# Routing by expert choice: the router product with its matrix held in TensorE, and the threshold search with the next two candidates made ahead

## The reference, cut to what matters

```python
xt = layernorm(x).reshape(N, D)                 # N = 8192, D = 128
scores = softmax(xt @ Wr, axis=-1)              # Wr: 128 x 8
G, idx = top_k(scores.T, k)                     # k = 2048 tokens of each expert
X_in = xt[idx]
h = gelu(einsum('ekd,edh->ekh', X_in, W1) + b1)
X_e = einsum('ekh,ehd->ekd', h, W2) + b2
out = zeros.at[idx].add(G * X_e)
```

## Time and profile before

| | |
|---|---|
| median of 3 runs | 3967.55 us (3966.43 to 3967.9) |
| the profiled execution, its own time | 3959.59 us |
| its span in the profile | 3957.4 us |
| its mean granted TensorE clock | 0.94 of full speed |
| TensorE busy over the span | 3411.8 us (86%) |
| VectorE busy | 2894.6 us (73%) |
| ScalarE busy | 1895.0 us (48%) |
| GpSimd busy | 1550.7 us (39%) |

### The profile page before, as it was taken

One profiled execution on the slowest core, in us unless ns is written; L12 is line 12 of the kernel. 1 busy time (PEld: TensorE's weight loads), 2 busy tenths in 40 slices (PEclk: granted clock), 3 DMA queues, 4 the chain that ended last, 5 costly groups with the idle time before them and its releaser, 6 DMA issues. The chain is left out here.

```text
span 3957.4 us, 60589 instructions
## 1 busy us (share of the span) xinstructions
PE 3411.8 (86%) x21076; PEld 2116.3 (53%) x21076; DVE 2894.6 (73%) x6400; ACT 1895.0 (48%) x3447; POOL 1550.7 (39%) x1015
## 2 busy tenths in 40 slices
PE   5999999878999984677748888888886999999987
PEld 3666666555777764344423333333333666666653
DVE  7888888556777755533239999999997777777765
ACT  2555556324665650222237676776673333333325
POOL 2311111542211200588848878878873011111112
PEclk9999999998999995798969999999998999999999
DMA  6333332004444424233332332322322222222211
GB/s 151 94 89 90 89 89 57 1 5 113 101 101 103 98 62 123 58 43 44 42 79 73 95 99 83 94 78 73 95 78 60 90 87 87 87 87 87 88 59 43
DMA packets 242528, 314.18 MB, mean 79 GB/s; under 512 B 46450, under 2 KB 157779, under 8 KB 231588
## 3 DMA queue, kind: packets, MB, share of 16 engines
q1 hardware_dynamic: 208308, 289.02, 26.6%
q0 software_dynamic: 22528, 17.32, 3.3%
q10 hardware_dynamic: 11392, 3.97, 0.5%
HBM read 251.93 MB, written 57.08 MB: 78 GB/s over the span
## 5 line engine op out<-in xcount | busy, mean ns | idle before, releaser
L574 DVE TENSOR_REDUCE a_Mx<-a_Sx 128x2 f32<-128x512 f32 (+1 forms) x1024 | 590.2, 617 | 173.4 <-PE a_Sx L626 128.0
L2187 POOL TENSOR_TENSOR a_inp<-a_dtu,a_Bs 128x1024 f32<-128x1024 f32 x256 | 598.0, 2361 | 68.6 <-DMA a_Bs<-a_brows 43.4
L2465 DVE TENSOR_TENSOR_SCAN a_h<-a_dA,a_inp 128x1024 f32<-128x1024 f32 x256 | 583.0, 2283 | 32.1 <-ACT a_dA L2348 28.7
L2592 PE MATMUL a_Y<-a_hc,g_ident 128*128 128x512 f32 x1024 | 487.6, 599 | 5.4 <-POOL a_hc L2201 3.6
L347 POOL TENSOR_TENSOR a_rest<-a_qk,a_parts 128x512 f32<-128x512 f32 x64 | 75.3, 1176 | 917.0 <-ACT a_parts L399 917.0
L413 ACT ACTIVATE a_Pr<-a_SA 128x512 f32<-128x512 f32 x512 | 305.1, 596 | 167.7 <-DVE a_SA L524 79.6
L623 PE MATMUL a_Sx<-att_Kp,att_Qp 96*128 96x256 bf16 (+1 forms) x2048 | 345.8, 261 | 41.4 <-DMA att_Qp<-a_crows 18.1
L2348 ACT ACTIVATE a_dA<-a_dtA,a_A 128x512 f32<-128x512 f32 x512 | 329.8, 681 | 97.8 <-DVE a_h L2465 96.8
L1937 ACT ACTIVATE f_sg<-f_GB 128x512 f32<-128x512 f32 x272 | 162.7, 598 | 436.5 <-PE f_GB L2013 436.3
L2063 PEld LDWEIGHTS f_OUT<-g_routed_wd,f_hm 128*128 128x128 f32 x2176 | 280.6, 191 | 124.1 <-issue 90.5
L2592 PEld LDWEIGHTS a_Y<-a_hc,g_ident 128*128 128x128 f32 x1024 | 195.4, 194 | 234.0 <-issue 222.7
(11 more groups left out here) (474 smaller groups left out, 6803.3 us busy)
## 6 DMA issues: line engine op xcount, KB each, us to landing
a_Bs<-a_brows SPq DMA_DIRECT2D x256, 256.0 KB, 3.3
f_Cs<-f_crows SPq DMA_DIRECT2D x512, 128.0 KB, 2.9
att_Qp<-a_packing SPq DMA_DIRECT2D x192, 192.0 KB
att_Kp<-a_packing SPq DMA_DIRECT2D x192, 192.0 KB
a_packing<-a_parts SPq DMA_DIRECT2D x64, 384.0 KB, 2.8
a_packing<-a_parts SPq DMA_DIRECT2D x64, 128.0 KB, 2.8
a_Cs<-a_brows SPq DMA_DIRECT2D x32, 256.0 KB, 4.7
g_x<-x SPq DMA_DIRECT2D x8, 512.0 KB, 7.4
```

The source lines that it names most:

```text
L574: nc.vector.tensor_reduce(Mx[(k + 2 - (j < LATE)) % 2][:, t, 2 * jj:2 * jj + 2], Sx[t][:, 0:2 * wd].rearrange("p (h q) -> p h q", h=2), AX ...
L2187: nc.gpsimd.tensor_tensor(inp[n % Q][:], dtu[k][:], Bs[n % Q][:].unsqueeze(1).to_broadcast([P, CH, GT]), ALU.mult).then_inc(s["mulB"], 1)
L2465: nc.vector.tensor_tensor_scan(h[n % 2][:].rearrange("p c q -> p (c q)"), dA[m % 2][:].rearrange("p c q -> p (c q)"), inp[n % Q][:].rearra ...
L2592: nc.tensor.matmul(Y[c][:], ident[:], hc[n % Q][:, c], start=False, stop=(n == N - 1))\
```

## The change

In the router, the roles of the two operands are exchanged. `wr` (128 rows, 8 columns) becomes the stationary operand and the 512 tokens of `xnT` are streamed past it in one matmul into a new PSUM tile `LT` of 8 partitions x 512. ScalarE copies `LT` into a new SBUF tile `rows`. TensorE turns the four 8 x 128 pieces of `rows` back with four transposes against the 8 x 8 corner of the identity, into the old places of `LG`, one step later than the old matmuls were. VectorE's copy of `LG` moves by one step too, and the loops of both engines get one step more (`back=1`).

In `choose`, there are two buffers `cand`. While the counts of one candidate are being added, VectorE brings `kth` up to date for the bit before (`copy_predicated`), and makes both next candidates: `high`, for the case that the bit is taken, and the other `cand` buffer, for the case that it isn't. When the sum is there, it makes the mask and copies `high` over the new candidate where the mask is set.

```diff
+        LT = [sc.ps(f"LT{i}", [E, GT]) for i in range(2)]
+        rows = [sc.sb(f"rows{i}", [E, GT]) for i in range(2)]
...
         def _(act):
...
                 if on(1):
                     wait(act, xn_used, g + 2)
-                    wait(act, lg_mm, g)
+                    wait(act, lt_mm, g)
                     nc.scalar.activation(xnT[(k + 1) % 2][:], T[(k + 1) % 2][:], ACT.Copy).then_inc(xt_ready, 1)
+                if on(0):
+                    wait(act, lt_mm, g + 1)
+                    wait(act, lg_mm, g - 1)
+                    nc.scalar.activation(rows[k][:], LT[k][:], ACT.Copy).then_inc(rows_ready, 1)
...
         def _(pe):
...
                 if on(0):
                     wait(pe, xt_ready, g + 1)
-                    wait(pe, copied, g - 1)
+                    wait(pe, rows_ready, g - 1)
+                    nc.tensor.matmul(LT[k][:], wr[:], xnT[k][:], start=True, stop=True).then_inc(lt_mm, 1)
+                if on(-1):
+                    wait(pe, rows_ready, g)
+                    wait(pe, copied, g - 2)
                     for t in range(G):
-                        last = nc.tensor.matmul(LG[k][:, t * E:t * E + E], xnT[k][:, t * P:t * P + P], wr[:],
-                                                start=True, stop=True)
+                        last = nc.tensor.transpose(LG[(k + 1) % 2][:, t * E:t * E + E],
+                                                   rows[(k + 1) % 2][:, t * P:t * P + P], ident[0:E, 0:E])
                     last.then_inc(lg_mm, 1)
-            straight(pe, step, GROUPS, 2)
+            straight(pe, step, GROUPS, 2, back=1)
...
         def _(v):
...
-                if on(0):
-                    wait(v, lg_mm, g + 1)
-                    nc.vector.tensor_copy(wts[:, bass.ds(g * G, G), :],
-                                          LG[k][:, 0:G * E].rearrange("p (t e) -> p t e", t=G)).then_inc(copied, 1)
-            straight(v, step, GROUPS, 2)
+                if on(-1):
+                    wait(v, lg_mm, g)
+                    nc.vector.tensor_copy(wts[:, bass.ds((g - 1) * G, G), :],
+                                          LG[(k + 1) % 2][:, 0:G * E].rearrange("p (t e) -> p t e", t=G)).then_inc(copied, 1)
+            straight(v, step, GROUPS, 2, back=1)
...
             nc.vector.memset(kth[:], 0)
+            nc.vector.memset(cand[0][:], 1 << (BITS - 1))
             v.wait_ge(turned, 1)
             then(nc.vector.tensor_copy(s[:], TT[:]))
             for b in range(BITS):
-                then(nc.vector.tensor_scalar(cand[:], kth[:], 1 << (BITS - 1 - b), None, ALU.bitwise_or))
-                nc.vector.tensor_scalar(junk[:], s[:], cand[:].bitcast(F32), None, ALU.is_ge, ALU.add,
+                now, after = cand[b % 2], cand[(b + 1) % 2]
+                nc.vector.tensor_scalar(junk[:], s[:], now[:].bitcast(F32), None, ALU.is_ge, ALU.add,
                                         accum_out=cnt[:]).then_inc(counted, 1)
+                if b:
+                    then(nc.vector.copy_predicated(kth[:], mask[:], after[:]))
+                if b < BITS - 1:
+                    bit = 1 << (BITS - 2 - b)
+                    nc.vector.tensor_scalar(high[:], now[:], bit, None, ALU.bitwise_or)
+                    then(nc.vector.tensor_scalar(after[:], kth[:], bit, None, ALU.bitwise_or))
                 v.wait_ge(total, b + 1)
                 then(nc.vector.tensor_scalar(mask[:], CT[:, 0:1], float(K), None, ALU.is_ge))
-                then(nc.vector.copy_predicated(kth[:], mask[:], cand[:]))
+                if b < BITS - 1:
+                    then(nc.vector.copy_predicated(after[:], mask[:], high[:]))
+                else:
+                    then(nc.vector.copy_predicated(kth[:], mask[:], now[:]))
```

More of the change, by code:

```diff
@@ L1460, in router_scores @@
         LG = [sc.ps(f"LG{i}", [P, 512]) for i in range(2)]
-        loaded, xn_ready, xn_used, xt_ready, lg_mm, copied, seq, exped = (
-            sc.sem(n) for n in "loaded xn_ready xn_used xt_ready lg_mm copied seq exped".split())
+        LT = [sc.ps(f"LT{i}", [E, GT]) for i in range(2)]
+        rows = [sc.sb(f"rows{i}", [E, GT]) for i in range(2)]
+        loaded, xn_ready, xn_used, xt_ready, lt_mm, rows_ready, lg_mm, copied, seq, exped = (
+            sc.sem(n) for n in "loaded xn_ready xn_used xt_ready lt_mm rows_ready lg_mm copied seq exped".split())
         block = ctx.enter_context(nc.Block())
@@ L1545, in choose @@
         s, junk, eq, pre = (sc.sb(n, [P, BL, P]) for n in ("s", "junk", "eq", "pre"))
-        kth, cand, mask = (sc.sb(n, [P, 1], U32) for n in ("kth", "cand", "mask"))
+        kth, high, mask = (sc.sb(n, [P, 1], U32) for n in ("kth", "high", "mask"))
+        cand = [sc.sb(f"cand{i}", [P, 1], U32) for i in range(2)]
         cnt, need = sc.sb("cnt", [P, 1]), sc.sb("need", [P, 1])
```

## The result

| | before | after |
|---|---|---|
| median | 3966.43 us (3963.03 to 3968.48, 9 runs) | 3955.70 us (3951.97 to 3959.12, 9 runs) |
| the profiled execution, its own time | 3959.59 us | 3959.12 us |
| its span | 3957.4 us | 3956.8 us |

The ratio is 0.9977, with an interval of 0.9968 to 0.9985: 9.1 us less (5.9 to 12.7). That is faster by a little more than the 0.2% that this kernel's measurement can tell. The forecast was 13.9 us less, 3953.5.

What follows compares the result with a forecast made beforehand. It took TensorE at 1.2 GHz to bound the router loop, and VectorE and TensorE waiting in turn to bound the search rounds. Router -8.4 and search -5.5 gave -13.9 us, from 3967.55 to 3953.5; range 3949 to 3978.

Steps and rivals of the forecast that it cites:

- The clock: Router loop: TensorE's granted clock rises from 0.50 to 1.00 within 3 to 7 us of the first transposes; 62 in 100.
- the clock that stays low: Router loop: TensorE stays at 1.2 GHz throughout; kernel +9.1 us, 3976.6; 30 in 100.
- What a us at the low clock costs: Router loop: each us that TensorE spends at the low clock before the rise costs 0.5 us.
- The router term: Router loop: with the clock raised after 5 us, 31.4 us against 39.8, so -8.4 us; bounds -6 and -10.
- The handoffs: Router loop: every handoff between engines has a step of slack, so none falls inside a step.
- rival 2: Router loop: ScalarE's copies and the products wait in turn, the step stays near 2.45 us; 3963.5; 5 in 100.
- The search term: 30 search rounds: the candidate leaves the chain, 0.18 us less each, -5.5 us in all; bounds -2.5 to -5.8.
- rival 3: Search rounds: the work ahead isn't hidden, they give 2.5 us instead of 5.5; 3956.5; 3 in 100.
- The rival's price: Router loop at 1.2 GHz: a step of 3.35 us instead of 2.45, loop +14.6 us; 30 in 100.
- The sum: Whole kernel: router -8.4 and search -5.5 give -13.9 us, from a median of 3967.55 to 3953.5.

Runs made afterwards that it cites:

- serial kernel: The changed kernel without the step of slack: transposes, copy, product, copy and transposes back of one group per step; 3989.01 us, ratio 1.0085 to the kernel before.
- one-wait kernel: The changed kernel without VectorE's wait after the operation that makes the new candidate in the search; 3942.94 us, ratio 0.9972 to the kernel before.

## Why the prediction was right, and where its sizes were off

**The clock: right.** It rose on the new loop's dense opening and stayed. The forecast was 3 to 7 us after the first transposes, 5 in the sum; the profiles of kernels with the plain new loop have 6.1, 4.6, 2.9 and 3.4. The chance of 30 in 100 for the clock that stays low hung on whether a stationary of 8 columns and 128 rows counts. With it the clock rose in these four, and read 1.00 from there on. The matmuls with 32 rows and 16 columns that raised nothing aren't of that kind, and no run varied rows and columns apart. That those ran at the low clock is read from their durations alone: the profile's clock column says 1.00 from 6.8 to 20 us, where the four matmuls of line 782 take twice what they take later (2.05 us, then 1.03). What part the transposes have in it isn't shown either: the old loop, in which the clock fell after four matmuls, differs from the new one in its transposes and in its passes, and no run varied one of them alone.

**What a us at the low clock costs: right.** The forecast said 0.5 us. Rises after 2.9, 3.4, 4.6 and 6.1 us went with loops of 31.8, 32.0, 32.7 and 33.3 us: 1.5 / 3.2 = 0.47.

**The router term, -8.4: too large by 0.4 to 2.** The four loops give -8.0 to -6.5 against 39.8, and the changed kernel's own profile the smallest. The bounds of -6 and -10 held. Two sizes were off. The step was 1.88 instead of 1.78: the sum of part prices has no pause between transposes and product, and the trace has 0.59 for transposes that I priced at 0.46 and 0.95 for passes at 0.86, while the transposes back were cheaper (0.34 instead of 0.46). Over 13 steps that is 1.3 us. And in the profile the rise came 1.1 us later, which is 0.5 us. Together 1.8 of the 1.9 us between 31.4 and 33.3.

**The handoffs: right.** No wait for ScalarE or VectorE stands in the full raised steps, and rival 2 is out. The serial kernel shows what the slack of a step is worth.

**The search term, -5.5: too large by 2.0, the one step whose reasoning failed.** The text said that the copy feeds the count, "so nothing is added", and that the work ahead fits under 0.68 us of cover with 0.1 to spare. The work fits more easily than that: one-column operations that don't depend on each other start 0.07 us apart, and 0.38 us of idle time was left before the mask, not 0.1. What I hadn't counted is that the work ahead ends in a wait of its own, which stands directly before the wait for the total. It costs 0.07 us a round and 29 x 0.07 = 2.0 us in all, while the engine is idle anyway. The one-wait kernel takes it back, 56.5 us against 58.6. The bounds of -2.5 to -5.8 held, but for a reason (longer gaps) that wasn't the one, which is luck. The sign named for rival 3, a mask later than 0.68 us after the accumulator, did appear (0.76), with 3.5 us gained where that rival had 2.5; yet the work ahead was hidden, and it is the wait that wasn't. (30 x 0.18 is 5.4, not 5.5; this changes nothing.)

**The rival's price: about right, by two errors that cancel.** The transposes back cost 0.13 each at the low clock, not 0.205, but the transposes with the pause behind them and the product took 1.04 and 1.81 us, not 0.82 and 1.70: 1.04 + 1.81 + 0.52 = 3.37 us by the measured parts, 3.35 forecast. The clock rose, so nothing of the result hangs on it.

**The sum.** -13.9 was forecast; by stage it was -10.0 in the profile, and -9.1 (5.9 to 12.7) and -11.5 (7.5 to 15.4) in the two timed sets. The time of 3955.7 is only 2.2 us from the 3953.5 forecast, in part by luck: the kernel before came out at 3966.43, 1.1 us under the 3967.55 that the forecast started from, and the difference of the two medians, 10.7, is larger than the ratio's 9.1. The two errors add up to 3.9 us, and both were of the same kind: durations were added as if an engine passed from one piece to the next for nothing.

## What to carry to other kernels

An engine that is busy all the time can still be slow by its clock, as TensorE was here, busy 37.75 of 38.00 us at a granted clock of 0.50: read the granted clock of the stage beside the busy share, and where it is low, try another form of the same work. Exchanging the operands so that few loads carry many moving columns gained here although a step's sum of prices at equal clock (1.46 us for the old form and 1.88 for the new at 1.00) spoke against it, and only because the stages stood a group apart; in the serial order the kernel lost 33.6 us. Start times of two executions aren't comparable by themselves (1472.1 to 1476.8 us for the same loop): count from the last point that the change can't have moved. Work made ahead in an engine's idle time must not end in a wait right before the wait that matters, which made a round 1.95 us here instead of 1.88; let one wait cover both.

## What the runs showed of the hardware that was not expected

- Two waits in a row on VectorE cost 0.07 us even with the engine idle (0.70 against 0.63 us from the sum's start to the mask). On TensorE, two waits less changed nothing (step 1.88 both times).
- With the old router loop TensorE was busy for 37.75 of 38.00 us at a granted clock of 0.50, and when four matmuls had raised the clock ahead of it, it fell again 5.3 us into the loop (one execution).
- TensorE pauses when it passes from the four transposes to a product with 512 moving columns: its load of the new stationary starts 0.17 us after the last load before it ends, at a granted clock of 1.00. The old loop shows no such pause between its transposes and its short passes (1.46 us for 12 operations, 0.12 each, at 1.00).
- In three of twelve profiles, one of them with the old loop and the old search, ScalarE stalled several times at the first GELUs of the expert stage, some 11 us in all, with no releaser that explains it. By the total times of one profile each, the change would have been worth nothing.
